# Attention and FFN block: a re-ordered prelude, batch 1 later, the product with V in two steps, maxima 8 slots ahead

## The reference

```python
Q = X @ W_q.T
K = X @ W_k.T
V = X @ W_v.T
...
Qr = _rope(Qh, cos, sin)
Kr = _rope(Kh, cos, sin)
scores = jnp.einsum('bhqd,bhkd->bhqk', Qr, Kr) * DH ** (-0.5)
...
pattern = jax.nn.softmax(scores, axis=-1)
heads = jnp.einsum('bhqk,bhkd->bhqd', pattern, Vh)
...
xq = fake_quant_fp8(x)
wq = fake_quant_fp8(weight)
...
x = x + _L0_attn_ref(xn, ...) + _L0_ffn_ref(xn, ...)
```

## Time and profile before

| | |
|---|---|
| median of 3 runs | 465.14 us (465.06 to 466.79) |
| the profiled execution | 465.83 us |
| its span | 463.4 us |
| TensorE's granted clock over the span | 0.963 of full |
| first product for the maxima | 37.92 us |
| first scores for the exponents (slot 0) | 63.30 us |
| last exponents' product with V | 447.86 us |
| a settled batch, as 214 to 263 us | 49 us |

### The profile page before, as it was taken

One profiled execution on the slowest core, in us unless ns is written; L12 is line 12 of the kernel. 1 busy time (PEld: TensorE's weight loads), 2 busy tenths in 40 slices (PEclk: granted clock), 3 DMA queues, 4 the chain that ended last, 5 costly groups with the idle time before them and its releaser, 6 DMA issues.

```text
span 463.4 us, 9406 instructions
## 1 busy us (share of the span) xinstructions
PE 408.1 (88%) x2911; PEld 232.8 (50%) x2911; DVE 356.8 (77%) x1372; ACT 278.6 (60%) x505; POOL 282.0 (61%) x284
## 2 busy tenths in 40 slices
PE   7906769988979998999899989999899999999976
PEld 7505534443545555565456545655555454454434
DVE  2987677999698877887788868887888778778313
ACT  2655755565764675577656665575656746656741
POOL 2675763457677678467856765778657755234750
PEclk9956897997999999999999999999999999999999
DMA  8759117533367149604853375525662387020111
GB/s 284 248 170 214 36 60 178 111 55 115 99 108 138 37 129 206 124 15 145 198 116 49 114 193 105 93 71 173 124 137 70 130 169 139 3 91 2 47 47 45
DMA packets 34049, 53.16 MB, mean 115 GB/s; under 512 B 4496, under 2 KB 30480, under 8 KB 31120
## 3 DMA queue, kind: packets, MB, share of 16 engines
q1 hardware_dynamic: 34000, 52.57, 46.1%
HBM read 35.52 MB, written 16.78 MB: 113 GB/s over the span
## 4 chain that ended last, share of the span: by engine, by line
PE 60%; DVE 16%; ACT 8%; issue 7%; DMA 4%; POOL 3%; SPq 1%; DVEq 0%; ACTq 0%; POOLq 0%
PE o_ps L931 14%; PE st_ps L844 12%; PE s_ps L864 9%; PE m_ps L829 7%; DVE scratch L600 7%; PE m_ps L873 6%; PE m_ps L896 6%; ACT prob L712 4%; PE m_ps L880 2%; DMA xnT<-x_dram 2%; PE m_ps L901 1%; DMA q_st<-shift 1%; DVE amax L538 1%; DVE rowmax L600 1%; PE m_ps L887 1%
## 5 line engine op out<-in xcount | busy, mean ns | idle before, releaser
L600 DVE CUSTOM_DVE_ANT_0 scratch<-s_ps,causal 128x512 bf16<-128x512 f32 (+3 forms) x512 | 220.4, 483 | 49.3 <-PE s_ps L864 49.0
L712 ACT ACTIVATE prob<-st_ps 128x512 f32<-128x512 f32 x320 | 175.0, 602 | 122.7 <-PE st_ps L844 122.0
L458 POOL TENSOR_SCALAR_AFFINE_SELECT prob<-prob 128x512 f32<-128x512 f32 (+1 forms) x160 | 90.2, 566 | 140.8 <-ACT prob L712 140.6
L864 PE MATMUL s_ps<-k_st,q_st 96*128 96x512 bf16 (+3 forms) x512 | 123.8, 304 | 23.8 <-DMA k_st<-qk_parts 14.3
L844 PE MATMUL st_ps<-q_st,k_st 98*128 98x128 bf16 (+3 forms) x512 | 123.8, 306 | 9.6 <-ACT prob L712 6.4
L931 PE MATMUL o_ps<-prob,v_sb 128*17 128x512 f32 (+3 forms) x1024 | 88.5, 440 | 1.2 <-POOL prob L458 0.7
L844 PEld LDWEIGHTS st_ps<-q_st,k_st 98*128 98x128 bf16 x512 | 40.4, 98 | 89.2 <-ACT prob L712 45.1
L864 PEld LDWEIGHTS s_ps<-k_st,q_st 96*128 96x128 bf16 x512 | 49.5, 99 | 51.4 <-DVE rowmax L600 16.7
L600 DVE DVE_READ_ACCUMULATOR2_ANT rowmax<- 128x1 f32 x512 | 40.8, 80 | 0.0
L931 PEld LDWEIGHTS o_ps<-prob,v_sb 128*17 128x17 f32 x1024 | 20.3, 96 | 39.4 <-issue 35.0
L313 POOL TENSOR_TENSOR parts<-rot,parts 128x1024 bf16<-128x1024 f32 (+1 forms) x16 | 32.6, 2041 | 2.4 <-ACT parts L698 2.4
(11 more groups left out here) (101 smaller groups left out, 514.1 us busy)
## 6 DMA issues: line engine op xcount, KB each, us to landing
qk_parts<-parts SPq DMA_DIRECT2D x16, 768.0 KB, 3.7
q_st<-qk_parts SPq DMA_DIRECT2D x15, 384.0 KB, 4.9
k_st<-qk_parts SPq DMA_DIRECT2D x15, 384.0 KB, 7.2
xnT<-x_dram SPq DMA_DIRECT2D x8, 512.0 KB, 8.7
q_st<-qk_parts SPq DMA_DIRECT2D x15, 256.0 KB, 3.8
k_st<-qk_parts SPq DMA_DIRECT2D x15, 256.0 KB, 8.3
x_res<-x_dram SPq DMA_DIRECT2D x7, 512.0 KB, 3.5
out_dram<-x_res SPq DMA_DIRECT2D x7, 512.0 KB, 3.0
```

The costliest lines, as they stand in the source:

```text
L458: eng.affine_select(out=ap, in_=ap, compare_op=ALU.is_ge, fill=0.0, base=0, pattern=pat, channel_multiplier=-1).then_inc(masked, 1)
L600: eng.tensor_tensor_reduce(scratch[:, at % 3, col:col + w], s_ps[at % 3][:, col:col + w], causal[:, T - w:T], 1.0, NEG, ALU.add, ALU.max, ...
L712: eng.activation(prob[u][:, half * T:(half + 1) * T], st_ps[ST_BANK[2 * s + half]][:, :], ACT.Exp, scale=SCALE).then_inc(exp_done, 1)
L864: mm = eng.matmul(bank[:, col:col + (qb + 1) * P], q_st[0:ROWS, n % 2, h, qb * P:(qb + 1) * P], k_st[0:ROWS, n % 2, h, 0:(qb + 1) * P], st ...
```

## The change

- `LEAD` is 8: maxima run 8 slots ahead of the exponents, the loop starts at slot -8.
- Both `v` items stand in slots 0 and 1, `mt` of group 1 in slot 2 (from 1), `mt` of group 0 in slot -3 (from -4).
- Batch 1: its four `qk` stand in slots -3, -2, 0 and 1 (from -10, -10, -7 and -5), its chain in the slots of `EARLY_CHAIN` (`rotate` 0 in slot -1, from -9; the last `low` in slot 4, from 0).
- `pv` has two steps: blocks of keys 1, 3 and 2 are one step, in slot 6 of the count (21 for the last group). `exp`, `copy_v` and `copy_heads` count accordingly.
- Prelude: x of batch 1 is loaded ahead of cos and sin, which have a semaphore of their own; the weights are split by ScalarE and GpSimd ahead of batch 0's chain; VectorE does all of `remainder` and `low` of batch 0; three statistics stand ahead of `rope` (from four), three behind, two in slots -8 and -6; the first write of q and k is three writes each, one per bf16 part (`write_first`); `fill_ones(1)` no longer waits for the chain of batch 1; `normalise` runs one batch further ahead.
- `keep_busy` does 22 and 6 products (from 26 and 8), and 20, 16 and 10 more ahead of slot -8, between which it waits for the last `low` and the last write.

```diff
-LEAD = 10
+LEAD = 8
...
-OFFSETS = {("v", 0): 0, ("mt", 1): 1, ("v", 1): 3, ("o", 0): 23, ("o", 1): 24, ("o", 2): 25, ("o", 3): 26, ("mt", 2): 7,
+OFFSETS = {("v", 0): 0, ("v", 1): 1, ("mt", 1): 2, ("o", 0): 23, ("o", 1): 24, ("o", 2): 25, ("o", 3): 26, ("mt", 2): 7,
...
-           ("qk", 2): -27, ("fin", 1): 34, ("at", 3): 34, ("qk", 3): -25, ("fin", 2): 36, ("mt", 0): -4, ("fin", 3): 38}
+           ("qk", 2): -27, ("fin", 1): 34, ("at", 3): 34, ("qk", 3): -25, ("fin", 2): 36, ("mt", 0): -3, ("fin", 3): 38}
 SPREAD = [(17, "spread", 0, 0), (18, "spread", 0, 1)]
-TURN_SLOT = {3: -10, 4: -9, 5: -7, 6: -5, 7: -3}
+EARLY = {("qk", 0): -3, ("qk", 1): -2, ("qk", 2): 0, ("qk", 3): 1}
+CHAIN = {("rotate", 0): -29, ("high", 0): -28, ("remainder", 0): -27, ("middle", 0): -26, ("low", 0): -25,
+         ("write", 0): -24, ("rotate", 1): -24, ("high", 1): -23, ("remainder", 1): -22, ("middle", 1): -21,
+         ("low", 1): -20, ("write", 1): -19, ("read", 0, 0): -18, ("read", 0, 1): -16, ("read", 1, 0): -12,
+         ("read", 1, 1): -11}
+EARLY_CHAIN = {("rotate", 0): -1, ("high", 0): -1, ("remainder", 0): 0, ("middle", 0): 0, ("low", 0): 1,
+               ("write", 0): 2, ("rotate", 1): 2, ("high", 1): 2, ("remainder", 1): 3, ("middle", 1): 3, ("low", 1): 4,
+               ("write", 1): 5, ("read", 0, 0): 3, ("read", 0, 1): 6, ("read", 1, 0): 8, ("read", 1, 1): 9}
+TURN_SLOT = {3: -LEAD, 4: -LEAD + 1, 5: -LEAD + 2, 6: -LEAD + 4, 7: -LEAD + 6}
...
-    items = [(max(SLOTS * n + off, -LEAD), order[kind, k], kind, n, k) for (kind, k), off in OFFSETS.items()
-             for n in range(NB) if (kind, n) != ("qk", 0)]
+    items = [(EARLY[kind, k] if (kind, n) == ("qk", 1) else SLOTS * n + off, order[kind, k], kind, n, k)
+             for (kind, k), off in OFFSETS.items() for n in range(NB) if (kind, n) != ("qk", 0)]
...
+def chain_at(slot, *step):
+
+    if slot == EARLY_CHAIN[step]:
+        return 1
+    return batch_at(slot, CHAIN[step], 2)
...
+            def write_first(w):
+
+
+                for t, (done, out_) in enumerate(((hi_done, early_out), (mid_done, early_out), (low_done, parts_out))):
+                    eng.wait_ge(done[w], 2)
+                    eng.dma_start(qk_dram[0, w].rearrange("t r j h n -> (j h) t r n")[:, t],
+                                  parts[:, w, t]).then_inc(out_[w], 16)
...
                 eng.wait_ge(parts_out[w], 16 * (n + 1))
+                if n == 0:
+                    eng.wait_ge(early_out[w], 32)
...
                 eng.dma_start(dst, src.rearrange("(c p) r m -> p c r m", p=P)).then_inc(w_qk_in, 16)
-            eng.dma_start(cos_sb[:, :], cos).then_inc(w_qk_in, 16)
-            eng.dma_start(sin_sb[:, :], sin).then_inc(w_qk_in, 16)
-            for n in range(1, NB):
+            load_x(1)
+            eng.dma_start(cos_sb[:, :], cos).then_inc(cos_in, 16)
+            eng.dma_start(sin_sb[:, :], sin).then_inc(cos_in, 16)
+            for n in range(2, NB):
...
             for w in range(2):
-                write_parts(0, w)
+                write_first(w)
...
-            for n in range(3):
-                invert(n)
+            invert(0)
+            split_weights(0)
+            invert(1)
+            split_weights(1)
+            invert(2)
             eng.wait_ge(ln_rstd, 6)
             fill_ones(0)
             eng.wait_ge(consts, 7)
-            remainder(eng, 0, 0)
-            low(eng, 0, 0)
-            split_weights(0)
-            split_weights(1)
...
-                if slot in (-9, -7):
-                    invert({-9: 6, -7: 7}[slot])
-                if slot == -4:
+                if slot in (-LEAD, -LEAD + 2):
+                    invert({-LEAD: 6, -LEAD + 2: 7}[slot])
+                if slot == -LEAD + 3:
                     eng.wait_ge(ln_rstd, 2 * NB)
-                    eng.wait_ge(low_done[0], 4)
                     fill_ones(1)
                     eng.wait_ge(consts, 9)
...
-            for n in range(4):
+            for n in range(3):
                 statistics(n)
-            eng.wait_ge(w_qk_in, 16 * 4)
+            eng.wait_ge(cos_in, 16 * 2)
             rope(0, 0, first_ps[0])
             rope(0, 1, first_ps[1])
             rotate(eng, 0, 0)
             rope(0, 2, first_ps[2])
+            remainder(eng, 0, 0)
             rope(0, 3, first_ps[3])
             rotate(eng, 0, 1)
+            low(eng, 0, 0)
             remainder(eng, 0, 1)
             low(eng, 0, 1)
-            for n in range(4, NB):
+            for n in range(3, 6):
                 statistics(n)
...
+                if slot in (-LEAD, -LEAD + 2):
+                    statistics({-LEAD: 6, -LEAD + 2: 7}[slot])
...
-                    eng.wait_ge(pv_done, 12 * n + 3 * (g - 1) + (1, 1, 2, 2, 3)[u])
+                    eng.wait_ge(pv_done, 8 * n + 2 * (g - 1) + (1, 1, 2, 2, 2)[u])
...
-                    wait_past(eng, pv_done, 12 * n)
+                    wait_past(eng, pv_done, 8 * n)
...
-                eng.wait_ge(pv_done, 12 * n + 3 * (g + 1))
+                eng.wait_ge(pv_done, 8 * n + 2 * (g + 1))
...
             normalise(0)
+            eng.wait_ge(w_qk_in, 16 * 2)
+            for parts_of, raw in zip(w_parts, (wq_sb, wk_sb)):
+                eng.copy(parts_of[:, 0], raw).then_inc(w_high, 1)
             copy_turned(0)
             normalise(1)
             normalise(2)
             high(0, 0)
             copy_turned(1)
             middle(0, 0)
+            copy_turned(2)
             high(0, 1)
             middle(0, 1)
-            for parts_of, raw in zip(w_parts, (wq_sb, wk_sb)):
-                eng.copy(parts_of[:, 0], raw).then_inc(w_high, 1)
             high_x(1)
-            copy_turned(2)
             normalise(3)
+            normalise(4)
...
-                    if n + 1 < NB:
-                        normalise(n + 1)
+                    if n + 2 < NB:
+                        normalise(n + 2)
...
-                for kb in ((0,), (1, 3), (2,))[step]:
+                for kb, us in (((0, (0, 1)),), ((1, (2, 3)), (3, (2, 3)), (2, (4,))))[step]:
...
-                    eng.wait_ge(masked, SLOTS * n + 5 * g + (2, 4, 5)[step])
-                    for u in ((0, 1), (2, 3), (4,))[step]:
+                    eng.wait_ge(masked, SLOTS * n + 5 * g + (2, 5)[step])
+                    for u in us:
...
-            keep_busy(26)
+            keep_busy(22)
             turn_rows(0)
-            keep_busy(8)
+            keep_busy(6)
             for k in range(4):
                 project_whole(k)
             turn_rows(1)
             turn_rows(2)
+            keep_busy(20)
+            eng.wait_ge(low_done[1], 2)
+            keep_busy(16)
+            eng.wait_ge(parts_out[1], 16)
+            keep_busy(10)
...
-                for off, g, step in ((20, 3, 1), (21, 3, 2)):
-                    n = batch_at(slot, off)
-                    if n is not None:
-                        pv(n, g, step)
+                n = batch_at(slot, 21)
+                if n is not None:
+                    pv(n, NG - 1, 1)
                 for g in range(NG):
-                    for off, step in ((3, 0), (5, 1), (6, 2)):
+                    for off, step in ((3, 0), (6, 1)):
```

26 lines of the change are left out of this document (15 added, 11 removed).

## The result

| kernel | median | ratio to the kernel before, 95% interval |
|---|---|---|
| before | 465.1 us | |
| changed | 472.72 us (470.31 to 473.37) | 1.0153 (1.0109 to 1.0197) |
| changed, timed again with other runs | 473.73 us (472.46 to 478.98) | 1.0198 (1.0132 to 1.0264) |

Forecast were 466.2 us and a range of 460.5 to 471.0: the change costs 7.6 us and the range does not hold it. The profiled execution took 473.16 us for a span of 471.4. One of the ten executions of late_exps_first, further down, took 798 us where the others took 463 to 467; it is in that kernel's median (464.3 us without it) and not in its ratio.

What follows compares the result with a forecast made beforehand. TensorE bounds settled batches, VectorE batch 0 from 78.0 to 111.7 us, nobody before that from 40.2. Terms -3.4 + 4.7 - 3.1 + 2.9 = +1.1 us gave 466.2 us; 8-in-10 range 460.5 to 471.

Steps and rivals of the forecast that it cites:

- The first stacks: Start of batch 0: first row maximum at 34.8 us in place of 40.24, gain 5.4 us, bounds 3.5 and 6.5.
- That SBUF rule: Prelude: two-input VectorE instructions contend only with GpSimd instructions reading SBUF, so rotation beside a memset has zero delay.
- the four edits: Prelude: fewer fill-in products, earlier rope, remainder and low on VectorE, smaller last write; together gain 5.4 us.
- From the first maximum to slot 5: Batch 0: slot 0 opens nearly 12 us earlier, a new 4.8 us wait before v; gain shrinks to 3.4 us.
- the clock term: Prelude to slot 6: TensorE at half clock behind its waits, cost 4.7 us, bounds 0 and 7.5.
- VectorE is full from there in both kernels, so the difference carries: Batch 0 from slot 5: the 3.4 us gained by then stays, 76.1 against 79.5.
- Terms two and three: Batch 0: gain of 3.4 us up to slot 5 and half-clock cost of 4.7 us.
- Settled batches: turn_heads waits less for the copy of v: gain 0.45 us a batch, 3.1 in all, bounds 0 and 7.4.
- The end: Last batch: moved V step, last product behind the last mask, more maxima; cost 2.9 us, bounds 1.0 and 4.3.
- (2): Rival: serial door in slots 0 to 4 decides, low clock and turn_heads waits, 472 us; 0.32 together with (3).
- serial door: Slots 0 to 4: batch 1's chain passes GpSimd and ScalarE among the first exponents, two rounds of 10.0 us.
- (3): Rival: at the start the reads of k land no earlier than 37.9 us; 469 us, 0.32 together with (2).

Runs made afterwards that it cites:

- late_exps_first: Kernel before with the re-ordered prelude, batch 1 late and its four ScalarE casts one slot later, behind the exponents: 464.83 us, ratio 0.9995.
- exps_first: Changed kernel with ScalarE's four casts of batch 1 one slot later, behind the exponents of their slot: 462.36 us, ratio 0.9947.
- reads_later: Changed kernel with the k reads of batch 1's first half issued in slot 8, behind the shift rows, not slot 6: 470.42 us, ratio 1.0101.
- fill_v_wait: Changed kernel with 16 fill-in products in TensorE's wait ahead of batch 0's second v: 467.94 us, ratio 1.0067.
- v_early_alone: Kernel before with the re-ordered prelude, the second v in slot 1 and group 1's maxima turn in slot 2: 455.87 us, ratio 0.9799.
- door_moved: v_early_alone with batch 1's writes, last cast and last low one slot later, and GpSimd's memset in slot 9: 456.35 us, ratio 0.9820.

## Why the prediction was wrong, step by step

- **The first stacks: right.** T = 34.82 us, forecast 34.8. That SBUF rule and the sum of the four edits held.
- **From the first maximum to slot 5: the waits right, the size short by 2 us.** Slot 0 opened at 52.9 us (forecast 51.5; a `qk` at 45.68 us took 2.82 us, at half clock, for which 0.9 was in the clock term), v at 63.3 (61.3) after 4.65 us (4.8), slot 5 at 80.6 (75.9 and 2.5 of clock, 78.4).
- **"VectorE is full from there in both kernels, so the difference carries": this step failed.** At slot 5 the changed kernel's exponents were 1.7 us late, at slot 9 4.0, at slot 10 7.2 and at batch 1's slot 0 7.1. Behind slot 5 VectorE was busy for 27.8 of 33.7 us and not for 33.3. It had stood idle before that, for scores that TensorE could not make while it waited for exponents (8.3 us in one piece, ahead of the fourth `qk`'s rope, and 3.53 us ahead of slot 5's maxima), half clock followed, and at slot 10 came the shift rows' 3.75 us. Only from slot 10 on does the difference carry as I had it. That VectorE was full before because TensorE had run ahead of it is my reading; exps_first, where it is nearly full again, agrees with it. Terms two and three together were forecast at +1.3 and came to +7.1 at batch 1's slot 0 in the trace; the 5.8 us between are nearly all of the 6.5 by which the forecast was short.
- **The reads past which the shift rows move: overlooked.** Of the moved chain I costed casts and rotations, not its DMAs. In the changed kernel the k reads come 1.5 us ahead of group 2's shift rows, and 3.2 of the 5.8 us appear at slot 10. Taking the reads away gave 2.1 us in the trace and 2.3 in the medians (reads_later).
- **The clock: right where it can be read.** v and `qk` at half clock cost 2.8 us (2.5 forecast; fill_v_wait). Slots 5 and 6 were at half clock too, as forecast, but no run prices the remaining 2.2 us of the term. That fill_v_wait won 4.8 us in the median, close to the 4.7 of the whole term, is no proof of it.
- **Settled batches: right as a sum, wrong in its terms.** From batch 2's slot 0 to batch 6's the changed kernel gains 2.2 us, 0.54 a batch (0.45 forecast). But v early gives 1.0 (v_early_alone), and the product in two steps takes half of it where v is early, which I had costed at next to nothing. That the sum came out near is luck.
- **The end: right**, 2.9 forecast; from batch 6's slot 5 (+4.7 us) to the end (+8.0) it lost 3.3 (2.6 from its slot 0), of them 1.09 at the last product as the rows of masks said. One small term has no working: eight products at 0.11 to 0.22 us are 0.9 to 1.8 us, and I took 0.4.
- **The rivals.** (2) named 472 us, and its point, slot 5 after 79.5 us, is where it went. Of its two causes one is true in part (half clock for v, the fourth `qk` and slots 4 to 6, but not for slots 2 and 3) and one isn't (`turn_heads` waits 2.5 us, not 7.4), so that it named the right number is luck. What none of the cases had is that the serial door starves VectorE behind slot 5. Rivals (2) and (3) shared 0.32; that four casts stand ahead of exponents, each with its wait for GpSimd, should have given (2) more.

## What to carry to other kernels

A gain or loss carries through a stretch where an engine was full only if what feeds that engine stays ahead: ask how far ahead its feeder runs after the change before you let a difference pass. On an engine that works in order, put what others wait for (exponents) ahead of what itself waits for a slow engine (a cast behind GpSimd); moving four casts by one slot was worth 10 us here, more than any other edit. And when a chain is moved, its DMAs move past others in the same queues: small transfers that someone waits for go ahead of large ones, and the next wait behind the one you remove decides what is won (4.47 us removed, 5.02 in its place, no gain).

## What the hardware showed that I had not expected

- Two rows of 4 KB take 1.8 us from issue to landing in the median, but 5.5 us to use when issued 1.5 us behind three reads of 768 KB in all, and 5.5 us again when issued 3.5 us behind such reads (door_moved). Issued ahead of them: under 2.3 us (reads_later). By the Trainium skill (DMA: Bandwidth & Descriptors, section Queues, rings and completion order) each DMA engine consumes a queue's descriptors in ring order; these rows agree in direction. The size doesn't go by the distance alone: in exps_first, 3.1 us behind the reads, it was 3.8 us (82.39 to 86.22).
- Executions of one kernel differ in how much of them runs at half clock: the two profiled executions of the changed kernel have a mean clock of 0.967 and 0.960 and spans of 471.4 and 473.1 us.
- Filling a wait of 4.65 us on TensorE with 16 products (3.7 us) kept the clock up for what followed (1.99 in place of 3.78 us for v); slot 5 opened 2.6 us earlier by it, and the median fell by 4.8. With a wait of 0.99 us the same products delayed v by 2.3 us, in a kernel that lost 1.7.
